# Window attention of layer 0: score products on 32 rows each, in two PSUM banks on top of the bias

## The reference, cut to what matters

```python
q, k, v = (proj(xw, Wq, bq), proj(xw, Wk, bk), proj(xw, Wv, bv))
qn, kn = q / norm(q), k / norm(k)
attn = einsum('whnd,whmd->whnm', qn, kn) * scale
attn = attn + bias[idx] + mask            # bias per head, mask per window position
attn = softmax(attn, axis=-1)
out = einsum('whnm,whmd->whnd', attn, v)  # then @ Wo.T + bo, added to x
```

## Time and profile before

| what | value |
|---|---|
| three runs | 1229.73, 1230.27, 1235.08 us; median 1230.27 |
| the profiled execution's own time | 1225.98 us |
| its span in the trace | 1224.1 us |
| mean granted TensorE clock over the span | 0.892 of 2.4 GHz |
| the loop of layer 0, from the first score product to the end of the last pair's scores | 79.2 to 247 us |

### The profile page before, as it was taken

How to read it: one execution, slowest core, us unless ns; L and a number is a source line. 1 busy time by engine, 2 the same in 40 slices (tenths; PEclk the granted TensorE clock), 3 DMA queues, 4 the chain that set the end, 5 groups by cost and what they waited for, 6 DMA issues and landing times.

```text
span 1224.1 us, 21611 instructions
## 1 busy us (share of the span) xinstructions
PE 957.1 (78%) x6752; PEld 575.7 (47%) x6752; DVE 814.1 (67%) x1680; ACT 697.4 (57%) x1287; POOL 645.7 (53%) x723
## 2 busy tenths in 40 slices
PE   5869999969997886678686555523999999999960
PEld 3435555534457452334353333311666666666640
DVE  7976666668848335667575444551877787787757
ACT  1815555544462557678564343212888888888850
POOL 3925555516778002003226555564677777777775
PEclk9969999979997997799898787655999999999985
DMA  5000000010023000001100000011011111111105
GB/s 202 1 2 1 1 2 1 2 65 1 1 80 104 0 1 1 1 2 29 48 7 22 20 20 20 19 44 40 26 35 31 34 33 32 35 30 36 30 24 204
DMA packets 24321, 39.37 MB, mean 32 GB/s; under 512 B 6212, under 2 KB 14168, under 8 KB 23960
## 3 DMA queue, kind: packets, MB, share of 16 engines
q1 hardware_dynamic: 15128, 28.62, 7.3%
q0 software_dynamic: 9088, 9.39, 2.4%
HBM read 24.52 MB, written 13.47 MB: 31 GB/s over the span
## 4 chain that ended last, share of the span: by engine, by line
PE 36%; POOL 18%; DVE 18%; issue 15%; ACT 8%; another core or an unknown queue 3%; SPq 1%; DMA 1%; POOLq 0%; DVEq 0%; ACTq 0%
POOL results L709 11%; POOL stage L721 7%; PE bank L1732 5%; PE bank L1743 2%; PE bank L1734 2%; PE bank L1808 2%; PE bank L1982 2%; PE bank L1757 2%; PE bank L1938 1%; PE bank L1961 1%; DVE T L807 1%; PE bank L1821 1%; PE bank L1856 1%; PE bank L1760 1%
## 5 line engine op out<-in xcount | busy, mean ns | idle before, releaser
L2175 PE MATMUL bank<-stage,big 128*114 128x512 f16 x936 | 243.2, 382 | 6.4 <-issue 3.1
L1339 DVE TENSOR_TENSOR T<-bank,T 114x512 f32<-114x512 f32 x234 | 161.5, 690 | 99.7 <-ACT T L1655 83.3
L686 POOL DMA_INDIRECT slots<-T,index x128 | 124.3, 971 | 121.0 <-DVE index L1250 84.5
L709 POOL DMA_INDIRECT results<-stage,small x156 | 153.1, 981 | 37.8 <-issue 37.8
L1655 ACT ACTIVATE T<-bank 114x512 f32<-114x512 f32 x234 | 139.7, 597 | 48.0 <-PE bank L2175 44.4
L2155 PEld LDWEIGHTS bank<-l2w,stage 114*128 114x128 f16 x1872 | 121.0, 98 | 56.2 <-issue 17.5
L1638 ACT ACTIVATE stage<-T 114x512 f16<-114x512 f32 x234 | 146.1, 625 | 0.3 <-DVE T L1339 0.3
L2155 PE MATMUL bank<-l2w,stage 114*128 x1872 | 143.6, 219 | 2.4 <-DVE stage L1349 1.4
L2175 PEld LDWEIGHTS bank<-stage,big 128*114 x936 | 107.9, 131 | 52.2 <-issue 14.6
L721 POOL TENSOR_TENSOR stage<-T,stage 114x512 f16<-114x512 f32 x78 | 89.9, 1153 | 55.7 <-ACT stage L1638 46.8
L1349 DVE TENSOR_TENSOR stage<-T,stage 114x512 f16<-114x512 f32 x156 | 106.4, 682 | 0.0
(11 more groups left out here) (386 smaller groups left out, 2007.9 us busy)
## 6 DMA issues: line engine op xcount, KB each, us to landing
stage<-slots SPq DMA_DIRECT2D x39, 130.0 KB
stage<-in_w1l SPq DMA_DIRECT2D x8, 342.0 KB
stage<-in_w3l SPq DMA_DIRECT2D x8, 342.0 KB
results<-stage,small POOLq DMA_INDIRECT x156
T<-in_xw SPq DMA_DIRECT2D x4, 512.0 KB, 6.0
X<-in_xi SPq DMA_DIRECT2D x1, 2048.0 KB, 14.6
slots<-T,index POOLq DMA_INDIRECT x128
A<-results SPq DMA_DIRECT2D x4, 512.0 KB, 6.7
```

Source lines behind the costliest of these rows:

```text
L686: pool.indirect_dma_start(slots_d, bass.IndirectOffsetOnAxis(ap=index[:, k, n:n + 1], axis=0), rows5[:, n * RW:(n + 1) * RW], None).then_i ...
L709: pool.indirect_dma_start(results_d, bass.IndirectOffsetOnAxis(ap=IDS[t % 4][:, i:i + 1], axis=0), Y5[t % 2][:, i, :], None).then_inc(S(f" ...
L1339: nc.vector.tensor_tensor(H5[q], bank[3 + q][0:HB, :], S5[q], ALU.mult).then_inc(S("hid5"), 1)
L2175: mm = nc.tensor.matmul(bank[q + 3 * (v // 2)][0:HB, :], big16[:, bass.ds(e * (4 * HID3) + (v * HID3 + k * HB), HB)], XT[s], start=(v % 2 ...
```

## The change

- The eight PSUM banks become one tensor, so that an access can run over two banks.
- POOL no longer builds QB. It builds a KX of 128 x 256: partition p keeps the keys for the slot h' (0 to 3) that is its head modulo 4. `slot_mask`, one small DVE operation at the start, is the mask for that. POOL waits for `k_norm` alone; PE waits for `q_norm` before the loop.
- `scores(n)` first writes bias and mask: four fp16 identity products of 256 columns, two for either of the two banks 2s and 2s + 1 (s = n % 2), columns 0 to 255 of each. Then come four fp32 products of 32 rows (partitions 64h + 32g on), 64 output partitions (64h on) and 256 columns, on top of the bias, into bank 2s + g. The queries are read from T1 in place.
- The maximum and the subtraction read 2 x 256 columns from the two banks.
- With four banks for scores there is one for the turned weights (bank 4, was 2), one for the sums (bank 7, was 2), and 5 and 6 for the values' results; the projection goes to 6. So `turn(n)` waits for the copy of pair n - 1 instead of n - 2, and the first `weigh` of a group waits for the logarithm of the sums before (`l0_lnsum`).
- `project_out` moves to k % 8 = 3 and behind `turn`, `invert_sums` to k % 4 = 1, `divide_group` to k % 4 = 2; `add_images` is split in five pieces at k % 8 = 3 and four at k % 8 = 4, and `image_stats` moves to k % 8 = 5.

```diff
@@ -162,7 +162,8 @@
         mats = sb("mats", [P, len(MATS), 128])
         vecs = sb("vecs", [P, len(VECS)])
         small = sb("small", [P, 1024])
-        bank = [ctx.enter_context(nc.psum_tensor(f"bank{i}", [P, CHUNK], F32)) for i in range(NCH)]
+        banks = ctx.enter_context(nc.psum_tensor("bank", [P, NCH * CHUNK], F32))
+        bank = [banks[:, i * CHUNK:(i + 1) * CHUNK] for i in range(NCH)]
 
         def mat(name):
             return mats[:, M[name], :]
...
@@ -201,8 +202,7 @@
         wv16 = l2w[:, 0:128].bitcast(F16).rearrange("p (v n) -> p v n", v=2)
 
         stage = sb("stage", [P, 4608])
-        QB = [stage[:, s * 128:(s + 1) * 128] for s in range(2)]
-        KX = [stage[:, 512 + s * 512:1024 + s * 512] for s in range(2)]
+        KX = [stage[:, 512 + s * 256:768 + s * 256] for s in range(2)]
         SC = [stage[:, 1536 + s * 512:2048 + s * 512] for s in range(2)]
         PR = [stage[:, 2560 + s * 512:3072 + s * 512] for s in range(2)]
         PT = [stage[:, 3584 + s * 512:4096 + s * 512] for s in range(2)]
...
-                pool.wait_ge(*when("q_norm", (NCH if not isinstance(n, int) else n // NWIN // 2 + 1)))
                 pool.wait_ge(*when("k_norm", (NCH if not isinstance(n, int) else n // NWIN // 2 + 1)))
 
                 reused(pool, "l0_scores", n)
-                nc.gpsimd.tensor_tensor(QB[s].rearrange("p (h q) -> p h q", h=2),
-                                        T1[:, bass.ds(n * WT, WT)].unsqueeze(1).broadcast_to([P, 2, WT]),
-                                        vec("half0", 2).unsqueeze(2).broadcast_to([P, 2, WT]),
+                nc.gpsimd.tensor_tensor(KX[s].rearrange("p (h k) -> p h k", h=HP),
+                                        T2[:, bass.ds(n * WT, WT)].unsqueeze(1).broadcast_to([P, HP, WT]),
+                                        slot_mask.unsqueeze(2).broadcast_to([P, HP, WT]),
                                         ALU.mult).then_inc(S("l0_staged"), 1)
-                nc.gpsimd.tensor_tensor(KX[s].rearrange("p (h k) -> p h k", h=HEADS),
-                                        T2[:, bass.ds(n * WT, WT)].unsqueeze(1).broadcast_to([P, HEADS, WT]),
-                                        hmask.unsqueeze(2).broadcast_to([P, HEADS, WT]),
-                                        ALU.mult).then_inc(S("l0_staged"), 1)
-
-            pool.wait_ge(*when("hmask", 1))
+
+            pool.wait_ge(*when("hmask", 2))
             steps(pool, stage_keys, 0)
...
                                     ALU.add).then_inc(S("hmask"), 1)
+            dve.wait_ge(*when("hmask", 1))
+            nc.vector.tensor_tensor(slot_mask, hmask[:, 0:HP], hmask[:, HP:HEADS], ALU.add).then_inc(S("hmask"), 1)
             nc.vector.tensor_copy(ident16[:, 0:128], mat("ident")).then_inc(S("ident16"), 1)
             nc.vector.tensor_scalar(lsc, vec("ls0"), float(np.log(np.float32(100.0))), None, ALU.min) \
...
@@ -826,29 +824,32 @@
 
             def shift_by_max(n):
                 s = n % 2
-                sc = SC[s].rearrange("p (h k) -> p h k", h=HEADS)
-                biased = bank[s][:, :].rearrange("p (h k) -> p h k", h=HEADS)
+                sc = SC[s].rearrange("p (g h k) -> p g h k", g=2, h=HP)
+                most = rowmax[s].rearrange("p (g h) -> p g h", g=2)
+                biased = banks[:, 2 * s * CHUNK:(2 * s + 2) * CHUNK].rearrange("p (g h k) -> p g h k", g=2, k=WT)[:, :, 0:HP, :]
                 dve.wait_ge(*when("l0_scores", n + 1))
-                nc.vector.tensor_reduce(rowmax[s], biased, AX, ALU.max).then_inc(S("l0_max"), 1)
+                nc.vector.tensor_reduce(most, biased, AX, ALU.max).then_inc(S("l0_max"), 1)
                 dve.wait_ge(*when("l0_max", n + 1))
                 if n >= 2:
                     dve.wait_ge(*when("l0_exp", n - 1))
-                nc.vector.tensor_tensor(sc, biased, rowmax[s].unsqueeze(2).broadcast_to([P, HEADS, WT]),
+                nc.vector.tensor_tensor(sc, biased, most.unsqueeze(3).broadcast_to([P, 2, HP, WT]),
                                         ALU.subtract).then_inc(S("l0_shifted"), 1)
 
             def divide_group(m):
                 dve.wait_ge(*when("l0_rsum", m + 1))
-                nc.vector.tensor_tensor(ch(T34, m), bank[4 + m % 2][:, :], RS[m % 2], ALU.mult) \
+                nc.vector.tensor_tensor(ch(T34, m), bank[5 + m % 2][:, :], RS[m % 2], ALU.mult) \
                     .then_inc(S("l0_out"), 1)
 
-            def add_images(c):
-                dve.wait_ge(*when("xi_biased", c + 1))
-                dve.wait_ge(*when("l0_wo", c + 1))
-                yw = bank[7][:, :].rearrange("p (b w i j) -> p b w i j", w=NWIN, i=WS, j=WS)
-                for wy, iy, r, nr in runs:
-                    for wx, ix, q, nq in runs:
-                        xv = Xi[:, 2 * c:2 * c + 2, r:r + nr, q:q + nq]
-                        nc.vector.tensor_tensor(xv, xv, yw[:, :, 2 * wy + wx, iy:iy + nr, ix:ix + nq], ALU.add)                             .then_inc(S("x1_ready"), 1)
+            def add_images(c, part):
+                if part == 0:
+                    dve.wait_ge(*when("xi_biased", c + 1))
+                    dve.wait_ge(*when("l0_wo", c + 1))
+                yw = bank[6][:, :].rearrange("p (b w i j) -> p b w i j", w=NWIN, i=WS, j=WS)
+                pieces = [(a, b) for a in runs for b in runs]
+                for (wy, iy, r, nr), (wx, ix, q, nq) in pieces[5 * part:5 * part + 5]:
+                    xv = Xi[:, 2 * c:2 * c + 2, r:r + nr, q:q + nq]
+                    nc.vector.tensor_tensor(xv, xv, yw[:, :, 2 * wy + wx, iy:iy + nr, ix:ix + nq], ALU.add) \
+                        .then_inc(S("x1_ready"), 1)
 
             def image_stats(c):
                 dve.wait_ge(*when("x1_ready", 9 * (c + 1)))
...
@@ -1407,13 +1408,13 @@
                 act.wait_ge(*when("l0_turned", n + 1))
                 if n >= 2:
                     act.wait_ge(*when("l0_pv", n - 1))
-                nc.scalar.activation(PT[n % 2], bank[2 + n % 2][:, :], ACT.Copy).then_inc(S("l0_pt"), 1)
+                nc.scalar.activation(PT[n % 2], bank[4][:, :], ACT.Copy).then_inc(S("l0_pt"), 1)
 
             def invert_sums(m):
                 act.wait_ge(*when("l0_pv", GROUP * (m + 1)))
                 if m >= 2:
                     act.wait_ge(*when("l0_out", m - 1))
-                nc.scalar.activation(RS[m % 2], bank[6 + m % 2][:, :], ACT.Ln).then_inc(S("l0_lnsum"), 1)
+                nc.scalar.activation(RS[m % 2], bank[7][:, :], ACT.Ln).then_inc(S("l0_lnsum"), 1)
                 act.wait_ge(*when("l0_lnsum", m + 1))
                 nc.scalar.activation(RS[m % 2], RS[m % 2], ACT.Exp, scale=-1.0).then_inc(S("l0_rsum"), 1)
 
@@ -1429,7 +1430,7 @@
                     exp_scores(k)
                 if 1 <= k <= PAIRS:
                     keep_turned(k - 1)
-                if k % GROUP == 2 and k >= 6:
+                if k % GROUP == 1 and k >= 5:
                     invert_sums(k // GROUP - 1)
                 if k % 8 == 4 and k < PAIRS:
                     add_bias(k // 8)
...
@@ -1726,21 +1727,29 @@
 
             def scores(n):
                 s = n % 2
-                pe.wait_ge(*when("l0_staged", (n + 1) * 2))
                 if n >= 2:
                     pe.wait_ge(*when("l0_shifted", n - 1))
-                nc.tensor.matmul(bank[s][:, :], QB[s], KX[s], start=True, stop=False)
-                for v in range(2):
-                    mm = nc.tensor.matmul(bank[s][:, :], ident16[:, 0:128], BM16[:, n % NWIN, v, :], start=False, stop=(v == 1))
+                for g in range(2):
+                    for v in range(2):
+                        nc.tensor.matmul(bank[2 * s + g][:, 0:HP * WT], ident16[:, 0:128],
+                                         BM16[:, n % NWIN, v, g * HP * WT:(g + 1) * HP * WT], start=(v == 0), stop=False,
+                                         skip_group_check=True)
+                pe.wait_ge(*when("l0_staged", n + 1))
+                for g in range(2):
+                    for h in range(2):
+                        r = 64 * h + 32 * g
+                        mm = nc.tensor.matmul(bank[2 * s + g][64 * h:64 * h + 64, 0:HP * WT],
+                                              T1[r:r + 32, n * WT:(n + 1) * WT], KX[s][r:r + 32, :],
+                                              start=False, stop=True, skip_group_check=True)
                 mm.then_inc(S("l0_scores"), 1)
 
             def turn(n):
                 s = n % 2
                 pe.wait_ge(*when("l0_exp", n + 1))
-                if n >= 2:
-                    pe.wait_ge(*when("l0_pt", n - 1))
+                if n >= 1:
+                    pe.wait_ge(*when("l0_pt", n))
                 for g in range(HP):
-                    mm = nc.tensor.transpose(bank[2 + s][:, g * 128:(g + 1) * 128],
+                    mm = nc.tensor.transpose(bank[4][:, g * 128:(g + 1) * 128],
                                              PR[s][:, g * 128:(g + 1) * 128], mat("ident"))
                 mm.then_inc(S("l0_turned"), 1)
 
```

(26 more changed lines are left out.)

## The result

| | kernel before | changed kernel |
|---|---|---|
| median, 20 runs each | 1232.38 us | 1235.92 us |
| lowest to highest | 1226.87 to 1235.08 | 1230.87 to 1240.03 |
| ratio, 95% interval | | 1.0029 [1.0017, 1.0041] |
| span of the profiled execution | 1224.1 us | 1233.2 us |
| the loop: start of the last value copy to the next layer's first product | 78.3 to 261.9: 183.6 | 77.3 to 262.1: 184.8 |

The change makes the kernel slower by 0.29%, 3.5 us of the median (2.1 to 5.1 by the interval). That is within the 0.5% called no change, and the median is inside the range of 1222 to 1246 (just above the 1226 to 1235 of the likeliest case), but the interval leaves out both an unchanged time and the 0.4 us less that was forecast.

The account below looks back on a forecast made before the run. PE's work (2.50 us per step) bounds the kernel before, the ring (5.04 per two steps) the changed one. Eight steps: 4 x 5.04 + 1.01 = 21.17 against 21.16; 8 x 0.01 - 0.5 gives 1230.27 - 0.4 = 1229.9 us, range 1222 to 1246.

Parts of the forecast that it names:

- the likeliest case: Whole kernel: the forecast of no change, 1229.9 us, with its own range of 1226 to 1235; 50%.
- the ring: Layer 0 loop: cycle of scores, DVE's maximum and subtraction, ACT's exponential and now copy, turn, weigh, next scores; once per two steps.
- the sum of the ring: Layer 0 loop: 2.66 us from scores to turn plus 2.38 of PE's work, 5.04 us per two steps.
- The new products: Score products in the loop: four side by side, 2 x 0.22 + 0.13 = 0.57 us, where one product took 1.06.
- the gain of 0.19 us per step: PE's work per plain loop step: 2.31 us after the change against 2.50 before.
- The 0.4 us of the second scores: Loop start at half clock: 0.4 us more saved in the shorter second scores, besides 0.6 in the first.
- The half microsecond at the end: Loop end: the last turn waits for a copy more, so it comes 0.5 us later.
- the rival of missed gaps: Loop: small waits on DVE or ACT, or the logarithm's 10 us, add 6 to 10 us, 1238; 10%.
- Products in pairs: Score products sharing a bank or output partitions don't overlap: 0.44 us per ring turn, 14 us more, 1244; 15%.
- one by one: Score products don't overlap at all: PE's work 3.63 us per step, 71 us more, 1301; 7%.
- PE's work stays the bound: Loop: the copy's wait doesn't bind, steps take 2.31 us, 13 us less, 1217; 15% for over 6 us.
- The clock did not fall: Rival for the loop: idling PE drops to 1.2 GHz, making the loop over 100 us longer; 3%.

Follow-up runs that it names:

- a_copy_first: Changed kernel with ACT copying the turned weights of pair k-1 before the exponential of pair k: 1217.54 us, ratio 0.9871 to the kernel before.
- b_one_turn_bank: Kernel before with all turned weights in one bank, so turn(n) waits for the copy of pair n-1: 1244.33 us, ratio 1.0092 to the kernel before.
- a_again: Changed kernel unaltered, timed and profiled a second time: 1185.01 us against 1182.45 for the kernel before, ratio 1.0018.
- a_one_product: Changed kernel with only one of four score products per pair left (rows 0 to 31): 1189.98 us in one execution, against 1185.01 for the changed kernel.

## Why the prediction was right or wrong

- **The mechanism was right.** The single bank for turned weights puts the copy, queued behind the exponential, into the ring; PE idles a few per cent, steps alternate (2.31 and 2.73 forecast, 2.34 and 2.78 measured), and what the products win is lost. `a_copy_first` and `b_one_turn_bank` show it from both sides.
- **The step that failed is the sum of the ring, "5.04 us, 2.52 per step".** It measured 5.12. Two terms, both taken from rows of another situation, were too small. The new products, taken as 0.57 from the weigh products' pieces, end 0.64 us after the bias when DVE waits for them (0.59 when PE goes on, in `a_copy_first`). The turn behind the copy took 0.14 + 0.63 = 0.77 from the copy's end; 0.05 + 0.66 = 0.71 had been taken from one turn at the loop's end that waited for the exponential alone. The bias, 0.54 and not 0.58, gave 0.04 back. Together these are 0.09; the ring is 0.08 longer per two steps, four times in eight steps: 0.3 us, which is 21.47 against 21.17, and 2.4 us over 64 steps. With it the forecast would have been some 2 us above the kernel before, on the side that was measured. That leaves some 1.5 us of the 3.5, which no run places. What the prediction had right in size, a loop within 1% of its old length, came because the gain of 0.19 us per step and the wait nearly cancel, and there a few hundredths in a term decide the sign.
- **Start and end.** The first maximum came 0.8 us sooner after the value copies (3.1 us behind the last one and not 3.9), 0.6 was forecast. The 0.4 us of the second scores did not show as forecast: from the last value copy to the ninth maximum it is 22.7 us, and 23.1 in `a_again`, against 23.1 before; the clock rose at about 82 us in the one and 84 in the other. The half microsecond at the end is there too: the last turn's weight load starts 2.68 us behind the last maximum's start and not 2.13, behind a copy (249.45 to 250.04). It was given back at once, since the last projection found the clock still high (granted 1.00 there, 0.63 in the kernel before): 1.10 us and not 1.63.
- **Beside the path.** The projection piece is 1.01 as taken. The waits of weigh for the logarithm, the image pieces and the statistics add at most a few hundredths: four turns of the ring and the projection, 4 x 5.12 + 1.01 = 21.49, leave nothing of the 21.47, so the rival of missed gaps is out.
- **The rivals.** Products in pairs and one by one are out by three runs. "PE's work stays the bound" was wrong for this change, but it is what `a_copy_first` does, and its forecast of 13 us was near the 15.9 measured (14.5 in the loop). The clock did not fall in the changed kernel.

## What to carry to other kernels

When a change takes work off the busiest engine, add up the ring that passes through the other engines as well, and count in it what is queued ahead of each awaited instruction on its own engine; here a bank given up put a copy into the ring, and two swapped calls on another engine took the loop from 184.8 to 169.1 us. Price a term from a row in the same situation: who waits for the piece's end, and behind which wait it starts. Small products of different rows and output partitions cost little more than one of them, and a change of shape on PE 0.10 to 0.15 us (bias 0.54 or 0.44, turn 0.59 or 0.44), so put work of one shape together. No run separates the change itself from the first weight load behind it.

## What the runs showed of the hardware that was not expected

Four fp32 products of 32 rows, 64 output partitions and 256 columns take 0.64 us until DVE starts on them, one alone 0.59. And with products left out the clock rose later: the windows of `a_one_product` (one product per pair) show PE busy for 19.75 of 20 us and the granted clock still at 1.2 GHz, until past 101 us, where the two profiled executions of the changed kernel were granted 2.4 GHz from about 82 and 84 us on.

```profile
80.00:100.00 20.00, 19.75 (x116) 9.70 (x114) 8.30 (x12) 6.03 (x11) 3.68 (x6) 0.50 0.00 1
100.00:104.00 4.00, 4.00 (x40) 2.00 (x32) 1.93 (x3) 2.41 (x5) 0.61 (x1) 0.80 0.01 2
```

The kernel with two products on the same partitions was at 1.2 GHz until past 92 us, the one with two in one bank only until about 88. Why the clock rose late was not tried, and these are single executions. The first eight steps of `a_one_product` took 26.35 us against 20.07 in `a_again`, some 6 us more, and those of the other two 23.52 and 21.19, so the whole times of these three say less than their pieces.
